# DLRM tower: the gathers wait for counts of TensorE's progress

## What is computed

```python
e = jnp.stack([tbl_0[ids[:, 0]], ..., tbl_26[ids[:, 26]]], axis=1)        # 512 x 27 x 128
interactions = jnp.einsum('bnd,bmd->bnm', e, e)
i, j = jnp.triu_indices(27, k=1)
z = interactions[:, i, j]                                                   # 351 pairs
h = jnp.concatenate([z, dense_ctx], axis=1)                                 # 512 x 367
h = jnp.maximum(h @ W_top1 + b_top1, 0.0)                                   # 512
h = jnp.maximum(h @ W_top2 + b_top2, 0.0)                                   # 256
y = h @ W_top3
```

## Time and profile before

| | us |
|---|---|
| median of 3 runs (127.47 to 128.09) | 127.55 |
| the profiled execution | 128.7 |
| its span in the trace | 126.9 |

### The profile page before, as it was taken

The page is one execution under the profiler, slowest core; times in us unless marked ns, Lnnn a source line. Parts: engine busy times, 40 slices in busy tenths (PEclk is TensorE's granted clock), DMA queues, the critical chain, the costliest instruction groups (busy, mean ns, idle before and its releaser), DMA issues.

```text
span 126.9 us, 2434 instructions
## 1 busy us (share of the span) xinstructions
PE 105.5 (83%) x994; PEld 88.0 (69%) x994; DVE 73.5 (58%) x80; ACT 70.9 (56%) x101; POOL 64.9 (51%) x72
## 2 busy tenths in 40 slices
PE   5958996399996899996962799949997789999793
PEld 5927874178883678673751798929995689799591
DVE  2399981999979999599910494024134032541230
ACT  4399931999959999699990258112220243051021
POOL 2187873875838877568885257642573600001300
PEclk9999999959999999999999599996899999999999
DMA  1997987249886386673271025741253114203300
GB/s 40 324 371 167 282 278 223 97 74 300 219 245 258 73 284 144 266 236 120 62 287 44 26 82 162 159 141 35 86 155 64 41 41 140 41 5 140 57 5 1
DMA packets 12919, 18.32 MB, mean 144 GB/s; under 512 B 7601, under 2 KB 8190, under 8 KB 12908
## 3 DMA queue, kind: packets, MB, share of 16 engines
q1 hardware_dynamic: 9408, 12.77, 32.9%
q0 software_dynamic: 2048, 4.13, 12.1%
q10 hardware_dynamic: 1452, 1.27, 3.1%
HBM read 16.39 MB, written 1.77 MB: 143 GB/s over the span
## 4 chain that ended last, share of the span: by engine, by line
PE 48%; ACT 28%; issue 11%; DMA 7%; another core or an unknown queue 2%; DVE 1%; SPq 0%; ACTq 0%
PE psG L373 15%; PE psG L354 15%; ACT hot L565 10%; ACT parts L560 6%; ACT hot L572 5%; PE psG L400 5%; PE psH L417 4%; DMA pick_ids<-in_picked_ids 4%; PE psT L331 3%; PE psH L354 3%; ACT ET L543 3%; DMA pair_grams<-gram 2%; PE psH L385 2%; ACT ET L548 2%
## 5 line engine op out<-in xcount | busy, mean ns | idle before, releaser
L313 POOL DMA_INDIRECT rows<-in_tbl,ids_sb x62 | 62.6, 1009 | 37.1 <-issue 17.0
L354 PE MATMUL psG<-hot,parts 128*128 128x512 f32 (+1 forms) x196 | 50.7, 406 | 8.1 <-DVE hot L479 3.3
L354 PEld LDWEIGHTS psG<-hot,parts 128*128 128x128 f32 x196 | 36.1, 194 | 19.6 <-issue 7.6
L479 DVE TENSOR_TENSOR hot<-pick_ids,psH 128x1536 fp32r<-128x1536 int32 (+3 forms) x24 | 41.7, 1780 | 9.2 <-PE psG L354 3.4
L373 PE MATMUL psG<-ET 128*54 128x54 f32 x512 | 19.4, 232 | 8.5 <-issue 8.5
L373 PEld LDWEIGHTS psG<-ET 128*54 128x54 f32 x512 | 17.0, 147 | 11.2 <-issue 10.5
L565 ACT ACTIVATE hot<-pick_ids,row_no 128x512 fp32r<-128x512 int32 (+1 forms) x31 | 19.8, 702 | 3.2 <-DMA pick_ids<-in_picked_ids 2.5
L579 ACT COPY gram<-psG 128x432 f32<-128x432 f32 x8 | 7.3, 910 | 23.5 <-PE psG L373 23.5
L486 DVE TENSOR_TENSOR parts<-table,parts 128x512 fp32r<-128x512 f32 (+1 forms) x24 | 17.1, 753 | 0.0
L494 DVE COPY gram<-psG 128x432 f32<-128x432 f32 x8 | 7.2, 904 | 16.1 <-remote 9.5
L572 ACT ACTIVATE hot<-hot 128x1536 fp32r<-128x1536 f32 (+2 forms) x12 | 15.1, 1259 | 0.3
(11 more groups left out here) (29 smaller groups left out, 46.3 us busy)
## 6 DMA issues: line engine op xcount, KB each, us to landing
table<-in_tbl SPq DMA_DIRECT2D x6, 640.0 KB
table<-in_tbl SPq DMA_DIRECT2D x6, 512.0 KB
pick_ids<-in_picked_ids SPq DMA_DIRECT2D x11, 256.0 KB
rows<-in_tbl,ids_sb POOLq DMA_INDIRECT x62
pair_grams<-gram SPq DMA_DIRECT2D x4, 216.0 KB, 2.3
pair_grams<-gram ACTq DMA_DIRECT2D x4, 216.0 KB, 2.8
w_sb<-in_w SPq DMA_DIRECT2D x1, 768.0 KB
w_sb<-in_w SPq DMA_DIRECT2D x1, 512.0 KB
```

The costliest lines, as they stand in the source:

```text
L313: pool.indirect_dma_start(out=rows[:, n % RING, x, :], out_offset=None, in_=gathered_tables[f], in_offset=bass.IndirectOffsetOnAxis(ap=ids ...
L354: last = pe.matmul(picked_psum(k), parts[:, k % 2, x, c, :], hot[:, k % 2, c, looked_up(k)], start=x == 0 and c == 0, stop=x == 1 and c == ...
L479: dve.tensor_tensor(hot[:, k % 2, first:end, looked_up(k)], pick_ids[:, k % TABLES, looked_up(k)].unsqueeze(1).to_broadcast(shape), number ...
```

## The change

A new semaphore `progress` is raised by TensorE four times in each pick (in the middle and at the end of either half; the last but one matmul stands for the end, since the last one raises `picked`), once in each of the two banks of a unit (behind the eighth of its 16 matmuls), and once or twice in the parts of the layers. Gathers 0 to 3 are free. From gather 4 on each waits until `progress` has reached its number in the table `PROGRESS_AT`. The 19 waits for whole steps are gone; the ring's waits stay. The order of TensorE's matmuls, and of all instructions on the other engines, is as before.

```diff
-    BEHIND_PICKS = [8, 11, 14, 17, 21, 24, 29, 33, 37, 42, 48, 51]
-    BEHIND_UNITS = [44, 45, 53, 54, 60]
-    BEHIND_LAYERS = [57, 59]
+    PROGRESS_AT = [0, 0, 0, 0, 1, 2, 3, 4, 5, 7, 8, 9, 10, 12, 13, 14, 15, 16, 17, 18, 20,
+                   21, 22, 23, 24, 25, 26, 27, 28, 29, 30, 31, 32, 33, 34, 35, 36, 37, 38, 39, 40,
+                   42, 43, 44, 45, 47, 48, 49, 51, 52, 53, 54, 56, 56, 58, 58, 60, 61, 62, 63, 64, 66]
...
+        progress = sem("progress")
...
                 for x, f in enumerate(fs):
-                    if number in BEHIND_PICKS:
-                        pool.wait_ge(picked, BEHIND_PICKS.index(number) + 1)
-                    if number in BEHIND_UNITS:
-                        pool.wait_ge(multiplied[H - 1], 2 * (BEHIND_UNITS.index(number) + 1))
-                    if number == BEHIND_LAYERS[0]:
-                        pool.wait_ge(l1_done, N1)
-                    if number == BEHIND_LAYERS[1]:
-                        pool.wait_ge(l2_done, N2)
+                    if PROGRESS_AT[number] > 0:
+                        pool.wait_ge(progress, PROGRESS_AT[number])
                     pool.indirect_dma_start(
...
                         last = pe.matmul(picked_psum(k), parts[:, k % 2, x, c, :], hot[:, k % 2, c, looked_up(k)],
                                          start=x == 0 and c == 0, stop=x == 1 and c == CH[k] - 1)
+                        if c == CH[k] // 2 - 1 or c == CH[k] - 1 - x:
+                            last.then_inc(progress, 1)
                 last.then_inc(picked, 1)
...
                             if x == GB - 1:
                                 last.then_inc(multiplied[h], 1)
+                            if x == GB // 2 - 1 and h == H - 1:
+                                last.then_inc(progress, 1)
...
+                        if c == 0:
+                            last.then_inc(progress, 1)
                     if n % 2 == 1:
                         last.then_inc(l1_done, 1)
...
                     if c == NC - 1:
                         last.then_inc(l1_done, 1)
+                    elif n == N1 - 1:
+                        last.then_inc(progress, 1)
...
                     if k == end:
                         last.then_inc(l2_done, 1)
+                    elif k == first:
+                        last.then_inc(progress, 1)
```

## The result

The changed kernel takes 123.06 us (median of 4 runs, 122.75 to 123.58) beside 127.82 for the kernel before in the same session: ratio 0.962 [0.954, 0.969]. The forecast was 119.9 with a range of 114.5 to 128.0 and 0.80 on "faster". The sign and the range hold, and so does the part of the mechanism that gives the gain.

A forecast was written before the change was run, and what follows sets the result against it. TensorE carries 48% of the chain, ACT 28%, "issue" 11%, with waste beside runs of gathers. Terms 4.0 + 1.5 + 0.7 + 1.5 = 7.7 us took the median 127.55 to 119.9; range 114.5 to 128.0.

The forecast's parts named there:

- The signs that I had named: Units 0 and 1 under 6 us, POOL idle before single gathers, ACT's pick copies closer, clock 1.00 over unit 1.
- the signs against it: PE rows of 3 to 5 records between 1.1 us of "issue", more in units 2 to 5; or PE waiting for quad 16.
- Up to some 17 us: Waste claimed in picks and products, all beside runs of gathers: late TensorE signals and TensorE's unexplained idle time.
- The mechanism of the gain: At gathers: a held TensorE signal also holds GpSimd, so at most one or two are on the way; first landing frees TensorE.
- Units 0 and 1 (4.0): Products up to pick 10: 5.97 us lost, 4.0 gained as gathers 41 to 43 wait; bounds 6.0 and -1.
- the picks before them: Late signals of picks 1, 4 and 7: GpSimd stops earlier, hold-ups get shorter, 1.5 us gained; bounds 5.85 and -2.
- Units 2 and 3 (1.5): Products: 3.0 us lost, half of it gained as gathers 50 to 53 wait for later counts; bounds 3.0 and -1.1.
- Units 4 and 5 (0.7): Products: 2.2 us lost, 0.7 gained, gathers beside them staying about as dense; bounds 2.2 and -1.1.
- Signals and waits (0): TensorE's 84 added signals and GpSimd's 58 waits cost 0; gather 61 still in time for quad 16 by 1.5 us.
- The pauses were not the cure: Rival: each gather stalls TensorE wherever it stands, so little or no gain, 125.3 to 127.5 us; chance 0.17.
- Slower: the gathers arrive in the products: Rival: gathers 42 to 53 move beside units 1 to 3, late signals delay gather 61; 130.2, up to 134 us; chance 0.13.
- Much better: Rival: one wait per gather prevents hold-ups, all 17.0 us go: 110.5, with half the remainder 115.2; chance 0.12 under 116.

The follow-up runs named there:

- second execution: The changed kernel, unaltered, run and profiled once more against the kernel before: 122.92 us beside 127.78, ratio 0.961.
- g1_free_third: Changed kernel with all gather waits for TensorE's steps or counts removed, ring's waits kept, on a chip with hold-ups: 150.96 us, before 127.88, ratio 1.179.
- e3: Changed kernel with the new waits only up to gather 39, later gathers waiting as before the change: 107.92 us, ratio to before 0.9990.
- e4: Changed kernel with the new waits only from gather 40 on, earlier gathers waiting as before the change: 108.06 us, ratio to before 0.9992.
- e2_signals_only: Changed kernel with its 84 progress signals kept but the 19 old waits in place of the new ones: 108.09 us, ratio to before 1.0001.
- e1_free: Changed kernel with all gather waits for TensorE's steps or counts removed, ring's waits kept, on a chip without hold-ups: 107.99 us, ratio to before 0.9993.
- h2_plain_from_40: Kernel before with gathers 40 to 61 replaced by plain DMAs of the same 64 KB behind the same waits: 116.68 us, before 126.29, ratio 0.921.
- i2_paced_again: Changed kernel without gather waits for TensorE, a scratch memset between gathers instead, on a chip with hold-ups: 145.48 us, before 127.88, ratio 1.134.

## Why the prediction held, and where it was off

*The signs that I had named.* Not all came. Units 0 and 1 in under 6 us and a clock of 1.00 over unit 1: in the second execution (4.93 us, 1.00) and not in the first (8.02, 0.58). POOL's idle time before single gathers, ended by PE: yes, from gather 41 on. ACT's copies of picks 1, 4 and 7 closer behind their matmuls: in the first execution that of pick 1 is (0.5 us behind), that of pick 7 comes as soon as ACT is free, and that of pick 4 is further behind than before (3.4 us, was 2.3). Of the signs against it, short groups of records between "issue" of 1.1 us were still there (64.43 above, 81.75 in the second execution).

*What bounds.* Right: the waste was TensorE's signals and TensorE's own "issue" beside runs of gathers. "Up to some 17 us" of waste compares with 127.8 against 108.0 us on chips that have no hold-ups, 19.8.

*The mechanism of the gain.* Right in the part that gives it: a held signal now also holds GpSimd. With no wait for a step or a count the kernel takes 151 us (g1_free_third), with 19 it is 127.8, with 58 it is 123. The waits are a feedback. That the finer feedback gives the gain, and not the other places that some gathers have now, is my reading and not shown: the change does both, and e3 and e4, which could have told more, met no hold-ups. Wrong in two parts: that one or two gathers would be on the way at most, and that the first or last to land sets a signal free.

*Units 0 and 1 (4.0).* 1.36 in one execution and 4.45 in the other. Half of the 3.1 between them is idle time of TensorE inside the two units, 2.44 us against 0.93 in the rows of PE; the other half is the clock (windows: stretch, its us, busy of five engines, granted clock, DMA share, GB/s):

```profile
65.80:69.40 3.60, 3.52 (x79) 3.43 (x79) 2.18 (x3) 0.90 (x1) 1.88 (x2) 0.58 0.11 27
```
```profile
63.00:68.00 5.00, 3.95 (x128) 3.65 (x128) 1.28 (x2) 3.50 (x5) 2.77 (x4) 1.00 0.16 52
```

The first execution (upper) stalled longer in unit 0 and was then granted 0.58 of the clock, partly the lower level, over its last 79 records: 3.59 us where 27 ns each make 2.1, so 1.5 us. The second (lower) kept 1.00. With the picks before them (1.5 forecast, 2.66 and 0.92 measured) this part gave 4.0 and 5.4 of the 5.5 forecast. I had not seen that the gathers would lag behind their counts and that two of them would still run in unit 0.

*Units 2 and 3 (1.5).* 1.84 and 0.28; with picks 10 and 11 before them, 1.7 and -0.3. This term was far too large in one of two executions.

*Units 4 and 5 (0.7), layers of tile 0 (0).* Wrong each, right together. The two stalls in layers 1 and 2 (85.26 and 89.10 in the rows of after) are what unit 4 used to have, as the gathers now come earlier in TensorE's order. The layers lost 1.90 and 1.40, the units won 2.33 and 2.40: net 0.4 and 1.0.

*Behind unit 5 (0).* 0.55 given back in both, in layer 2 of tile 1, where TensorE now waits for ACT's result of layer 1. I had priced nothing there. In the first execution layer 1 ends at 96.62 + 2.84 = 99.46, and ACT starts on it only at 100.62, with gathers 59 to 61 started from 96.11 to 98.60; before, it ended at 105.60, 5 us behind the last gather, and ACT started at 105.64 (timelines of PE, ACT and POOL). I read it as a late signal of the same kind.

*The sum.* 2.1 of the 7.7 are missing in the first execution: 1.5 up to pick 10, 0.3 in units 4 and 5 with the layers and 0.55 behind unit 5, less 0.2 that came beyond the forecast around units 2 and 3. In the second it is 2.2, of which 1.8 around units 2 and 3. That the sum came as near as it did owes something to errors that offset each other. The terms that I would now make smaller are those of the products: I took the gathers beside them to be spread out, and gathers that lag behind their counts are as dense as before.

*Signals and waits (0).* Right: e2_signals_only. Gather 61 starts at 98.60, and quad 16 is transposed at 102.52 without idle time for it. My 2.6 us from the start of a gather to its landing were too few, if the 3.9 of e1_free hold here as well, but the slack of 1.5 us would have covered it.

*The rivals.* "The pauses were not the cure" fell: without them the kernel takes 151 us (g1_free_third). "Slower: the gathers arrive in the products" did happen: the negative rows of the table come to 2.6 us in both executions, in the layers more than in the products, and were outweighed. "Much better" fell for the reason in the rows of GpSimd: a wait for each gather doesn't mean that there is only one on its way.

*What was missing.* That the chip could be the variable. The chips seen fall into two kinds: before took 108.0, 108.0 and 108.3 us on three of them, and 126.3 to 127.9 on the others. No chip was seen in both kinds, but only one was met twice, so that the chip decides, and not the time of the run, is likely and not proved. My forecast was made from a trace with hold-ups and measured on a chip with them; on one without them it would have been wrong. That it wasn't is luck. The changed kernel itself was run only on the second kind; on the first, its two halves (e3, e4), its signals (e2) and no waits at all (e1) all lie within 0.4% of before, from which I infer that it gives nothing there.

**Still open.** What it is that takes 1.45 us for a gather, why some chips have it and others not, whether TensorE's own standstill in the products and its late signals are one thing, and how much of the gain the waits up to 39 and from 40 on each give on a chip that has hold-ups (e3 and e4 met none).

## What to carry to other kernels

Before a wait or a schedule is tuned against an unexplained "issue" or a late signal, run the kernel on several chips: what is worth 4% on one may be worth nothing on the next, and removing it may cost 18% there and nothing here. Where indirect DMAs of GpSimd run beside TensorE, let a gather wait for TensorE's progress, finely: on a chip with hold-ups it limits the backlog, and on one without it the two halves of the change cost nothing. Ask of each stretch by itself whether gathers come faster than they are worked off, and don't trust a split by stages from a single profile.

## What the runs showed of the hardware

- The same program took 108 or 151 us, depending on the chip, at a ratio to the kernel before of 0.9995 and 1.179.
- An indirect DMA of 128 rows (64 KB) is issued every 1.25 us (0.95 busy, 0.30 idle); on chips without hold-ups it lands 3.7 to 4.3 us after issue (median of each run). A plain one of the same size takes 0.54 us of GpSimd and lands after 2.3 us (h2_plain_from_40, on a chip with hold-ups). The Trainium skill ("Perfetto Trace Analysis", DMA Instruction — SWDGE (GPSIMD)) says that GpSimd's row ends with the making of the descriptors and not with the move; the 3.9 of e1_free beside 0.95 agrees.
- On the chips with hold-ups a hold-up ended about 1.45 us times the number of its gathers behind the first of them (1.41 to 1.47, groups of 7 to 40), and TensorE's signals, and in the products its own matmuls, were late until then.
- While DVE is at work some gathers take GpSimd 1.26 to 1.57 us in place of 0.95 (i2_paced_again); from 59.45 us on, with DVE mostly idle, all take 0.95.
